# Loads once for four chunks, and twice the row buffers in the second edge layer of a four-layer graph network

## What is computed

```python
def _L0_gnn_ref(h, weight, gate_weight, norm, src, dst, rel_type):
    h_all = jnp.einsum('nd,rdf->nrf', h, weight)
    gate_all = jnp.einsum('nd,rdo->nro', h, gate_weight)[..., 0]
    msg = h_all[src, rel_type] * norm
    gate = jax.nn.sigmoid(gate_all[src, rel_type])[:, None]
    msg = msg * gate
    out = jax.ops.segment_sum(msg, dst, num_segments=h.shape[0])
    return jax.nn.relu(out)

def _L1_gnn_ref(x, edge_index, edge_attr, timestamps, We1, be1, We2, be2, Wt, bt, Wn1, bn1, Wn2, bn2):
    ts = timestamps[:, None]
    ef = jax.nn.relu(edge_attr @ We1 + be1) @ We2 + be2
    tw = jax.nn.sigmoid(ts @ Wt + bt)
    ef = ef * tw
    combined = jnp.concatenate([x[row], ef], axis=1)
    msg = jax.nn.relu(combined @ Wn1 + bn1) @ Wn2 + bn2
    out = jax.ops.segment_sum(msg, col, num_segments=x.shape[0])
    return out + x
```

## Time and profile before

| | us |
|---|---|
| median of 3 runs | 7884.42 |
| lowest and highest run | 7872.66, 7892.95 |
| the profiled execution | 7896.64 |
| its span, from first to last instruction | 7894.2 |
| mean granted TensorE clock in it | 0.751 |

### The profile page before, as it was taken

The page is one execution under the profiler, slowest core; times in us unless marked ns, Lnnn a source line. Parts: engine busy times, 40 slices in busy tenths (PEclk is TensorE's granted clock), DMA queues, the critical chain, the costliest instruction groups (busy, mean ns, idle before and its releaser), DMA issues. The chain is left out here.

```text
span 7894.2 us, 105906 instructions
## 1 busy us (share of the span) xinstructions
PE 5657.7 (72%) x25772; PEld 3387.9 (43%) x25773; DVE 3166.8 (40%) x11018; ACT 2317.7 (29%) x5705; POOL 3138.5 (40%) x3263
## 2 busy tenths in 40 slices
PE   0766666566666654777777777777786996999999
PEld 0333333333333433444444444444453453444444
DVE  6566666666666654333333333333322112000000
ACT  0244444444444442232222222222211112111100
POOL 0265565556665562555555555555530000000000
PEclk9856555665656556777777777777767998999999
DMA  1322222222222222333333333333313443555555
GB/s 49 147 73 73 73 72 57 73 73 73 74 73 73 69 69 72 97 96 97 94 95 96 96 95 98 95 94 97 96 53 117 157 129 131 191 173 194 172 193 162
DMA packets 460919, 811.20 MB, mean 103 GB/s; under 512 B 218904, under 2 KB 233266, under 8 KB 457671
## 3 DMA queue, kind: packets, MB, share of 16 engines
q1 hardware_dynamic: 285148, 407.76, 16.6%
q0 software_dynamic: 103968, 213.28, 10.3%
q10 hardware_dynamic: 71728, 189.18, 7.4%
HBM read 697.44 MB, written 110.80 MB: 102 GB/s over the span
## 5 line engine op out<-in xcount | busy, mean ns | idle before, releaser
L613 POOL DMA_INDIRECT e_rows<-scratch_table,e_staged x1616 | 1583.3, 980 | 1364.1 <-DVEq L225 607.1
L1014 POOL DMA_INDIRECT e_rows<-scratch_table,e_staged x1616 | 1533.9, 949 | 1342.5 <-DVE e_z L1153 707.6
L549 PE MATMUL e_banks<-hi_hot,lo_hot 128*128 128x392 bf16 x3138 | 1073.0, 494 | 704.4 <-remote 314.4
L517 DVE TENSOR_SCALAR hi_hot<-iota_hi,key 128x392 bf16<-128x392 f16 x3138 | 1078.9, 344 | 16.7 <-issue 16.5
L160 PE MATMUL e_win<-e_onehot,e_msg 128*128 128x64 f32 x3232 | 562.3, 332 | 663.1 <-ACT e_msg L1096 645.9
L160 PEld LDWEIGHTS e_win<-e_onehot,e_msg 128*128 128x128 f32 x3232 | 542.6, 247 | 968.7 <-ACT e_msg L1096 825.5
L160 PE MATMUL e_win<-e_onehot,e_rows 128*128 128x64 f32 x3232 | 683.6, 386 | 282.1 <-issue 212.4
L549 PEld LDWEIGHTS e_banks<-hi_hot,lo_hot 128*128 128x128 bf16 x3138 | 354.7, 132 | 1227.4 <-issue 534.0
L160 PEld LDWEIGHTS e_win<-e_onehot,e_rows 128*128 128x128 f32 x3232 | 696.4, 306 | 413.7 <-issue 366.3
L516 DVE TENSOR_SCALAR lo_hot<-iota_lo,key 128x128 bf16<-128x128 bf16 x3138 | 783.3, 250 | 193.4 <-remote 156.0
L1324 PE MATMUL c_sums<-ring,parts 128*128 128x512 bf16 (+1 forms) x3822 | 789.8, 368 | 80.9 <-DMA c_bias<-in_conv_b 80.9
(11 more groups left out here) (188 smaller groups left out, 5767.1 us busy)
## 6 DMA issues: line engine op xcount, KB each, us to landing
ring<-scratch_counts SPq DMA_DIRECT2D x336, 896.0 KB, 4.7
e_time<-in_time_rows ACTq DMA_DIRECT2D x404, 256.0 KB
e_rows<-scratch_table,e_staged POOLq DMA_INDIRECT x3232
e_edge<-in_edge_T SPq DMA_DIRECT2D x202, 256.0 KB
scratch_counts<-h ACTq DMA_DIRECT2D x12, 3136.0 KB
scratch_counts<-type_mem ACTq DMA_DIRECT2D x12, 3136.0 KB
scratch_table<-table_tile SPq DMA_DIRECT2D x49, 512.0 KB, 2.6
e_staged<-idx SPq DMA_DIRECT2D x404, 2.0 KB
```

The source lines that it names most:

```text
L517: return nc.vector.tensor_scalar(hi_hot, iota_hi[:, :], key[:, 1:2], None, ALU.is_equal)
L549: return nc.tensor.matmul(bank, lo_hot[:, slot, :], hi_hot[:, slot, :], start=start, stop=stop)
L613: pool.indirect_dma_start(rows[:, b, j, :], None, A["table0"], bass.IndirectOffsetOnAxis(ap=staged[:, b, j:j + 1], axis=0),).then_inc(rows ...
L1014: pool.indirect_dma_start(rows[:, b, j, :], None, A["table1"], bass.IndirectOffsetOnAxis(ap=staged[:, b, j:j + 1], axis=0),).then_inc(rows ...
```

## The change

In both edge layers SP loads indices once for a round of four chunks, into one half of a double buffer, when the gathers of the round two back have landed; POOL waits once for each round. In the second layer the edge features and time rows of a round come in the same manner, from SP; ACT issues no loads, and both lie in `h`. The second layer's rows have eight buffers with semaphores of their own (`rows1_in`), and `z` of chunk c-8 frees one. After the gathers of every second chunk POOL waits until that chunk's rows have landed.

```diff
+        rows1_in = [root.enter_context(nc.semaphore(f"rows1_in{b}")) for b in range(2 * NB)]
...
-                staged = sbuf(st, "e0_staged", [P, NB, J], I32)
+                staged = sbuf(st, "e0_staged", [P, 2, NB * J], I32)
...
+                    def load(half, r):
+                        sp.dma_start(staged[:, half, :], idx8[:, bass.ds(r * (NB * J), NB * J)]).then_inc(index_in[half], 16)
+
+                    def reload(half, r):
                         for b in range(NB):
-                            sp.wait_ge(rows_in[b], base + 16 * J * o)
-                            load(b, o * NB + b)
+                            sp.wait_ge(rows_in[b], base + 16 * J * (r - 1))
+                        load(half, r)
...
-            rows = sbuf(st, "e1_rows", [P, NB, J, D])
-            staged = sbuf(st, "e1_staged", [P, NB, J], I32)
+            rows = sbuf(st, "e1_rows", [P, 2 * NB, J, D])
+            staged = sbuf(st, "e1_staged", [P, 2, NB * J], I32)
...
-            edge_in = sbuf(st, "e1_edge", [2 * EC, NB // 2, CH])
-            time_in = sbuf(st, "e1_time", [P, NB, CH])
+            inputs = h[:, :, :].rearrange("p t d -> p (t d)")
+            edge_in = inputs[:, 0:2 * NB * CH // 2].rearrange("p (k a e) -> p k a e", k=2, e=CH)
+            time_in = inputs[:, NB * CH:3 * NB * CH].rearrange("p (k b e) -> p k b e", k=2, e=CH)
...
+                def load(half, r):
+                    sp.dma_start(staged[:, half, :], src_idx[:, bass.ds(r * (NB * J), NB * J)]).then_inc(index_in[half], 16)
+                    sp.dma_start(edge_in[:, half, :, :], A["edge_T"][bass.ds(r * NB, NB), :, :]
+                                 .rearrange("(q a) k e -> (a k) q e", a=2)).then_inc(edges_in[half], 16)
+                    sp.dma_start(time_in[:, half, :, :].rearrange("p b e -> p (b e)"),
+                                 A["time_rows"].rearrange("(r b) e -> r (b e)", b=NB)[bass.ds(r, 1), :]
+                                 .to_broadcast([P, NB * CH])).then_inc(times_in[half], 16)
+
+                def reload(half, r, before):
+                    for b in range(NB):
+                        sp.wait_ge(rows1_in[half * NB + b], 16 * J * before)
+                    sp.sem_inc(s["begun"], 1)
+                    sp.wait_ge(s["p1"], (r - 1) * NB)
+                    sp.wait_ge(s["tw"], (r - 1) * NB)
+                    sp.sem_inc(s["begun"], 1)
+                    load(half, r)
...
+                def one_round(half, r, before, first):
+                    pool.wait_ge(index_in[half], 16 * before + 16)
                     for b in range(NB):
-                        gather(b, o * NB + b, o, False)
+                        if not first:
+                            pool.wait_ge(s["z"], r * NB + b - (2 * NB - 1))
+                        pool.sem_inc(s["begun"], 1)
+                        for j in range(J):
+                            pool.indirect_dma_start(
+                                rows[:, half * NB + b, j, :], None, A["table1"],
+                                bass.IndirectOffsetOnAxis(ap=staged[:, half, b * J + j:b * J + j + 1], axis=0),
+                            ).then_inc(rows1_in[half * NB + b], 16)
+                        if b % 2 == 1:
+                            pool.wait_ge(rows1_in[half * NB + b], 16 * J * before + 16 * J)
...
-                def load_time(c, b):
-                    act.dma_start(time_in[:, b % NB, :], A["time_rows"][bass.ds(c, 1), :]
-                                  .to_broadcast([P, CH])).then_inc(times_in[b % NB], 16)
```

More of the change, by code:

```diff
@@ L999, in _ @@
-                sp.dma_start(type_i[:, :], A["type_cols"]).then_inc(s["type_in"], 16)
-                for b in range(NB):
-                    load(b, b, None)
-                with sp.Fori(1, ROUNDS) as o:
-                    for b in range(NB):
-                        load(b, o * NB + b, o)
+                def load(half, r):
[5 more added lines that the diff above has]
+                                 .to_broadcast([P, NB * CH])).then_inc(times_in[half], 16)
@@ L1006, in _ @@
+                reload(0, 2, 1)
+                with sp.Fori(1, (ROUNDS - 1) // 2) as o:
+                    reload(1, 2 * o + 1, o)
+                    reload(0, 2 * o + 2, o + 1)
             @block.gpsimd
             def _(pool):
-                def gather(b, c, o, first):
-                    pool.wait_ge(index_in[b], o * 16 + 16)
-                    if not first:
-                        pool.wait_ge(s["z"], c - (NB - 1))
-                    pool.sem_inc(s["begun"], 1)
-                    for j in range(J):
-                        pool.indirect_dma_start(
-                            rows[:, b, j, :], None, A["table1"],
-                            bass.IndirectOffsetOnAxis(ap=staged[:, b, j:j + 1], axis=0),
-                        ).then_inc(rows_in[b], 16)
@@ L1024, in _ @@
+                one_round(0, 0, 0, True)
+                one_round(1, 1, 0, True)
+                one_round(0, 2, 1, False)
+                with pool.Fori(1, (ROUNDS - 1) // 2) as o:
+                    one_round(1, 2 * o + 1, o, False)
+                    one_round(0, 2 * o + 2, o + 1, False)
             @block.tensor
```

72 lines of the change are left out of this document (32 added, 40 removed).

## The result

| | before | after |
|---|---|---|
| median of 20 runs, us | 7885.55 | 7877.86 |
| lowest and highest | 7869.24, 7895.82 | 7764.17, 7959.06 |
| profiled execution, us (its span) | 7896.64 (7894.2) | 7885.54 (7883.6) |
| mean granted clock in it | 0.751 | 0.753 |

The ratio is 0.990, with a 95% interval of 0.9879 to 0.9922, where 0.967 was forecast. The ratio leaves out the ten of the 20 executions after that lie over 1.5% above the fastest (7885.5 to 7959.1 us, the profiled one among them), as slow ones; the other ten take 7764.2 to 7870.2. The medians differ by 8 us, the ratio by 1%, some 79 us; either is less than a third of the 259 us. What wasn't expected is the spread: before, all executions lie within 27 us; after, within 195 us.

A forecast was written before the change was run, and what follows sets the result against it. It took a second-layer loop of POOL's gathers, their landing, L199 and e_z, and POOL's restart as the bound. A pair going from 13.76 to 12.48 us saves 259 us: 7884.4 to 7625 us, range 7480 to 7940.

The forecast's parts named there:

- the 259 us: Forecast saving, all in the second layer: 1.28 us for each of 202 pairs of chunks.
- POOL's cycle of a pair: Second layer: eight gathers 9.67, landing 1.73, restart 0.78, sum 12.18 us, plus 0.3 for loads, against 13.76 before.
- Does compute keep up: Second layer: two e_z steps take 7.9 to 10.6 us, within POOL's 12.18, unless the hold falls in between.
- the hold: Second layer: a long run of POOL's gathers was read as delaying PE's completions to DVE until about the landing.
- the first rival's mechanism: Hold catches the second chunk's e_z, 5.2 us into POOL's run, between a free row (3.84) and a held one (5.6); chance 0.26.
- The rival's price: Second layer if the hold catches: 30.3 us a round against 27.5, 280 us more, 8165 us; chance 0.26.
- The loads of a round: Second layer, SP: index load covered by a full round, else some 2 us late; bulk data 0.3 us a pair.
- nothing changes: Rival: buffers serve nobody, or bulk loads delay one landing in two by 2.6 us; 7884 us, chance 0.16.
- The landing wait: POOL, second layer: not a price but the change's use, since without it runs of sixteen gathers and more would hold e_z.
- ACT's loads at nothing: Second layer: ACT no longer issuing 404 time loads is worth nothing; 137 us if ACT were on the path.
- The first layer at 0 within 30: First layer: index loads go from 404 to 101, already hidden, so zero gain, 30 us either way.
- The start: Second layer's start: the 13.68 us idle ahead of an early e_z would be gone; earlier index worth 2 or 3 us, left out.

The follow-up runs named there:

- e9: Changed kernel with SP's index load issued ahead of its waits for p1 and tw, in a session without holds: 7063.99 us, 1.0707 of the kernel before.
- e5: The changed kernel itself, run again in a session with holds: 7678.55 us, 0.9783 of the kernel before (7844.63 us).
- e17: The changed kernel once more, in another session with holds: 7689.36 us, 0.9805 of the kernel before.
- e13: Changed kernel, second layer in parts: A unchanged, B index first, C also data behind landing, D C with landing wait every chunk, E C without landing wait: 7841.88 us.
- e7: Changed kernel with edge and time loads waiting for the second pair's landing, in a session with holds: 7850.88 us, 1.0003 of the kernel before.
- e6: Changed kernel without POOL's landing wait after every second chunk, in a session with holds: 7942.99 us, 1.0117 of the kernel before.
- e18: Changed kernel with the index load ahead of SP's waits for p1 and tw, in a session with holds: 7715.33 us, 0.984 of the kernel before.
- e8: Second layer without indexed gathers: eight buffers, small loads, SP loads rows by plain transfers of the same size: 7011.99 us, 0.8933 of the kernel before.
- e15: Kernel before with eight row buffers and landing wait every second chunk, all loads small, with holds: 7711.4 us, 0.9832 of the kernel before.
- e16: Kernel before with eight row buffers, small loads and three lengths of POOL's gather runs in parts: 7819.65 us, 0.9976 of the kernel before.
- e14: Kernel before with eight row buffers, small loads and five manners of POOL's waiting in parts: 7956.94 us, 1.0086 of the kernel before.
- e4: Kernel before with only the first layer's index loads made once for four chunks, without holds: 6597.66 us, 0.9999 of the kernel before.
- e1: Kernel before with eight row buffers and landing wait every second chunk, all loads small, without holds: 7155.83 us, 1.084 of the kernel before.

## Why the prediction was wrong, by its own steps

That 7878 us lies in the range of 7480 to 7940 is no merit of the mechanism: the range was drawn so as to hold the unchanged time too. The 259 us didn't come, and these are the steps.

**POOL's cycle of a pair, 12.18 + 0.3 us: right where nothing else limits (12.36 us in e9), too small in the changed kernel.** In e5, where POOL sets the pace, a pair takes 13.05 us. The run of eight gathers was right (9.68 us for 9.67); the pauses, put at 1.73 + 0.78 + 0.3 = 2.81 us, are 2.71 and 3.68. With (13.05 - 12.48) x 202 = 115 us this is what e5 lacks of the stage's 259.

**"Does compute keep up": this step failed.** I put two steps of 3.94 to 5.31 us beside 12.18 us and said yes, as long as the hold doesn't fall in between. It does, in part of the pairs: e_z's unnamed waits went from 90 to 136, and from 139.6 to 383.1 us (353.7 in e5, 313.2 in e17). Compute fell behind until POOL, six or seven chunks ahead, waited for buffers (39 times, 91.5 us) and for indices that come from compute (36 times, 219.9 us). With the side paths removed (e13, C and E) POOL waits for e_z again. This is the first rival's mechanism, which had 0.26. Its place for the second e_z, 5.2 us into the run, was near: p3 was ready 5.9 us in, and was held. (The 0.67 us in that sum isn't what the rows give: L199 to e_z is 0.62 us, and L199 comes 0.01 to 0.30 us after the landing, so 5.2 to 5.5 us, still between the free row and the held one.)

**The rival's price was mis-sized.** I had every run caught, 30.3 us a round. Measured are 27.7 us a round (2795.8 / 403 x 4), 26.9 in the first half and 28.4 in the second, against 27.5 before; 26.1 in e5 and 26.3 in e17. A mean of caught and free pairs stands where I had either the one or the other. Whether a pair is caught depends on how far e_z lies into POOL's run, and the change has untied the two; before, e_z itself started the run.

**The loads of a round: two terms missed.** I counted the index load as covered by a whole round. It is queued on SP behind waits for p1 and tw, which come from the held compute; 36 times POOL waited for it, 219.9 us, some 6.1 us each or 3.7 more than a free pause of 2.4, where I had named 2. And the data, priced at 0.3 us a pair, made single landings as late as 7.16 us, 4.8 us more than the 2.4 of a free one; the upper bound of 5.8 us a round held. The data was named as a cause of "nothing changes", at 0.16 together with others; the index was named as a price alone. The data is what lengthens the pauses of e5, and taking either away gains little or nothing with holds: in e7 the index took the data's place (172 us slower than e5), and in e13's C, with both away, waits for buffers took their place (6.76 us a chunk for A's 6.84).

**The landing wait: right for this kernel, not as a rule.** e6 shows it to be worth 264 us with holds. In e13's C and E, with the loads moved, it is worth nothing (6.76 and 6.71 us a chunk). That it costs 463 us without holds no row of before could show.

**ACT's loads at nothing:** agrees, nothing in the waits points to them.

**The first layer at 0 within 30:** too sure. In the sessions with holds its last gather comes at 2897 to 2907 us with the new loads (e5, e6, e7, e17, e18) and at 2914 to 2921 with the old (e8, e15, e16), in e13 and e14 at 2925 and 2947, so 8 to 22 us within a session, and 33 in the pair of profiles. Without holds it is nothing (e4). How fewer small loads shorten a stage only where there are holds stays open.

**The start:** the 13.68 us ahead of an early e_z are gone; the longest unnamed wait of e_z is 6.7 us.

**The spread,** which I hadn't forecast: the parts of one execution run at 6.73 and 7.11 us a chunk, and the slow one is that in which POOL waits for the index. My reading is that executions differ in when they fall into that manner; 0.38 us x 404 = 154 us would cover most of the 195. What the traces add is POOL's distance ahead of e_z: three to five chunks throughout e5 (6.53 us a chunk), four and then six in e17 (6.57), six and seven in the slow half here, where the index is late. That executions differ by when they get there is argued, not shown: e5 and e17 never had a late index, no run forced it, and what moves an execution from four chunks to seven stays open.

Left open: what carries the hold, what switches it off in some sessions, and how much of the missing gain is compute's and how much the late landings', which differs from execution to execution. Of the versions that compute the same, none beats the changed kernel with holds, and none the kernel before without them.

## What to carry to other kernels

When two engines are untied by more buffers, look for every other wait that still ties them: here SP's index load behind tw and the hold itself did, and taking away one let the next fill its place. Count how far the one engine is ahead of the other: that, and not the name in a row of waits, tells whether it waits for the other. An engine that "keeps up on average" with 9.6 us of work in 12.2 can be late all the same if its results are delivered only in part of the cycle. And a wait that is there for a side effect is worth measuring wherever the kernel will run: the same line was worth 264 us in one session, and in another session it went with a loss of 463.

## What the runs showed of the hardware

- In sessions with holds, PE's results late in a run of indexed gathers on POOL reach DVE only about 1.2 us after the last gather ends (5555.47 to 5556.67). Runs of four are nearly free of it (4.7 us in 68 chunks), runs of five and six nearly so (0.36 us a chunk), runs of eight have 1.46. Plain transfers of the same size don't cause it (e8).
- The same kernel on a chip of the same number shows none of it in another session: 6598 us (e1 to e4) instead of 7845 (e5 to e8), with POOL gathering without a pause.
- A gather costs POOL 1.25 us from start to start, in either kind of session, which makes 5.02 us a chunk the floor of this layer; without gathers it is 4.81.
